# Summing the adjacency counts on VectorE before TensorE multiplies them, in a two-layer graph network

## The chip, the cores and the metric

One core of a Trainium2 chip. The metric is the device time of one execution in microseconds (us); lower is better. The kernel before takes 321.08 us, the median of 3 runs (320.94 to 321.26).

## What is computed

625 nodes of 512 features, 10000 edges (`src`, `dst`, each of one of 3 relations), nodes of 3 types. Layer 0 sums a message per edge, layer 1 is attention along the same edges with 8 heads of 64:

```python
h = maximum(layernorm(x), 0)
xr = einsum('nd,rde->rne', h, W_rel)
agg = segment_sum(xr[edge_type, src] + b_rel[edge_type], dst)
h_self = einsum('nd,tde->tne', h, W_self)[node_type, n] + b_self[node_type]
x = x + relu(h_self + agg)
h = maximum(layernorm(x), 0)
Q, K, V = split(h @ W_qkv.T + b_qkv)
att = softmax over the edges into each node of (Q[dst] . K[src]) / 8
x = x + segment_sum(att * V[src], dst) @ W_ff.T + b_ff
```

Two things are needed of the edges besides the messages: how many edges of each relation end in each node (the bias `b_rel` is added once for each), and, for the attention, how many edges run from each source to each target, whatever the relation (a pair with none is masked, and one with several gets the logarithm of their number).

## The kernel before, in words

The nodes are padded to NP = 640, five tiles (NT) of 128. The edges become a dense matrix of counts, `adjT[source in tile, source tile jt, relation r, target]`, fp16. It is built in 20 windows of 32 targets: VectorE (DVE) makes one-hot rows, `row_hot` (line 827) and `key_hot` (line 820), TensorE (PE) multiplies them (line 1083), and ScalarE (ACT) copies the window to `adjT` (line 523). Beside the windows runs a pipe for the self term (lines 1124 and 1130).

Then PE follows one list, `schedule`, written out by hand; ACT and DVE follow the same list, each doing its part of every unit in it. Units that use one of three PSUM banks in turn form the `ring`: a unit waits until DVE has freed the bank of the unit three places ahead of it (`take_bank`, semaphore `s_ufree`). The units around the change:

- `cnt`, two, one for each half of 320 target columns. PE writes the node types with 3 small matmuls (line 1162) and adds the counts by relation, 15 matmuls of 320 columns (line 1172): `sel6` sums over the sources within a tile, the 15 matmuls over tiles and relations. DVE copies the result to `cnt6` (lines 873 and 874), which meets the biases at line 1275.
- `z`, eight for each relation (4 groups of features, 2 halves): adjacency times features, 10 matmuls of 320 columns (line 1185). ACT takes the high part to `zT_even` or `zT_odd` (line 566), DVE the low part from the same bank (line 879) and frees it.
- `gemm`, five for each relation: 12 matmuls with `w_hl`, the two-part weights (line 1239).
- `m`, two for each target tile: `adjT` is turned over by multiplying it with an identity, 15 matmuls of 128 columns for a tile (line 1202), 12 in the first unit (4 source tiles, 512 columns) and 3 in the second (1 tile, 128 columns), which also sums over the relations. DVE makes `mcount` and `mask_add` (lines 893 and 895), ACT the logarithm (line 619), GpSimd (POOL) subtracts it (line 468).

The order is: `cnt` twice, `z` of relation 0, `z` of relation 1, then five times (`gemm` of relation 0, `m`, `m`), `z` of relation 2, the other gemms, the second layer.

Where a window needs over 16 chunks of edges (`pe.If(widest > EXACT16 // EL)`), counts may not fit fp16, and matmuls with the rest `adjT_res` are done too. With these edges the branch is skipped; its instructions are in the program.

ACT rounds the weights of relation 0, `w_hl` (line 514, `weights_hi`), after the last window, those of relation 1 ahead of its part of the first `z` unit of relation 1; POOL then makes the low parts, four operations each (line 439, `weights_lo`), and between the two it issues five gathers (line 457).

## Time and profile before

| | us |
|---|---|
| median of 3 runs | 321.08 |
| the profiled execution's own time | 321.26 |
| its span, first to last instruction | 319.5 |
| PE busy | 294.4 (92%) |
| DVE busy | 194.0 (61%) |
| ACT busy | 142.9 (45%) |
| POOL busy | 69.8 (22%) |

The granted TensorE clock is 1.00 of full speed (2.4 GHz) throughout. The chain that ended last is put down to PE for 81% of the span and to DVE for 12%. The windows fill the first 81 us, the stretch of `cnt` and the first 16 `z` units is 81 to 107.6 us, the gemms with `m` 107.6 to 126.7 us.

A duration in a row is the time an instruction is seen on its engine; two instructions of one engine overlap by a little, so that the distance from start to start is shorter.

### The profile page before, as it was taken

To read this page: it belongs to the slowest core of one execution; us is meant where nothing else is said; L and a number is where in the kernel's file an instruction comes from. 1 tells how busy PE (TensorE), PEld (TensorE's weight loads), DVE (VectorE), ACT (ScalarE), POOL (GpSimd) and SP (SyncE) were. 2 spreads that over 40 slices of the span, in tenths; PEclk is the share of its full clock that TensorE was granted. 3 is DMA by queue.
4 is the path that set the end of the run, shared out by engine and by line. 5 is a ranking of instruction groups with operands and counts; after the bars stand their busy time and mean duration, and the time that the engine had idled before them with its cause. 6 is when DMAs were issued, how large, how long until landed. Compare 5 with 4: busy or idle time off the path is not lost.

```text
span 319.5 us, 5460 instructions
## 1 busy us (share of the span) xinstructions
PE 294.4 (92%) x2006; PEld 226.4 (71%) x2006; DVE 194.0 (61%) x471; ACT 142.9 (45%) x282; POOL 69.8 (22%) x97
## 2 busy tenths in 40 slices
PE   2848699999999999998999999997999999999994
PEld 1513345544677788687887889997888898888882
DVE  5899977986234344334359744967857565565721
ACT  1152234523325322533343505687876464665621
POOL 6045003210655044800012402310002020020202
PEclk9999999999999999999999999999999999999999
DMA  5753992111080300045300000000000000000000
GB/s 181 251 209 131 331 386 106 67 36 55 17 291 8 133 2 2 2 131 139 125 0 0 2 0 3 0 3 0 2 0 2 36 0 35 1 2 35 1 35 29
DMA packets 10970, 22.29 MB, mean 70 GB/s; under 512 B 950, under 2 KB 966, under 8 KB 10938
## 3 DMA queue, kind: packets, MB, share of 16 engines
q1 hardware_dynamic: 8772, 16.80, 15.3%
q0 software_dynamic: 800, 2.62, 2.2%
q10 hardware_dynamic: 1366, 2.45, 2.1%
q8 instruction: 20, 0.33, 0.4%
q14 instruction: 12, 0.10, 0.1%
HBM read 15.60 MB, written 6.26 MB: 68 GB/s over the span
## 4 chain that ended last, share of the span: by engine, by line
PE 81%; DVE 12%; ACT 3%; issue 2%; DMA 1%; DVEq 0%; POOL 0%
PE banks L1239 15%; PE banks L1185 9%; PE banks L1225 9%; PE banks L1325 8%; PE banks L1130 8%; PE banks L1311 7%; PE banks L1300 7%; PE banks L1083 5%; PE banks L1345 5%; DVE key_hot L820 3%; DVE row_hot L827 2%; PE banks L1215 2%; PE banks L1335 2%; PE banks L1172 1%; PE banks L1202 1%
## 5 line engine op out<-in xcount | busy, mean ns | idle before, releaser
L1003 DVE CUSTOM_DVE_ANT_0 s_sb<-banks,mask_add 128x640 f32<-128x640 f32 x40 | 32.6, 822 | 22.2 <-PE banks L1300 22.1
L1083 PE MATMUL banks<-key_hot,row_hot 128*128 128x480 f16 x120 | 32.5, 419 | 9.0 <-DVE key_hot L820 9.0
L660 ACT ACTIVATE p_sb<-s_sb,neg_max 128x640 f32<-128x640 f32 x40 | 32.9, 823 | 17.3 <-DVE neg_max L1003 17.3
L820 DVE TENSOR_SCALAR key_hot<-iota,picked 128x480 f16<-128x480 f16 x120 | 36.9, 374 | 0.0
L1185 PE MATMUL banks<-adjT,h 128*128 128x320 f16 x240 | 33.1, 299 | 0.4 <-DVE zT_even L879 0.4
L1083 PEld LDWEIGHTS banks<-key_hot,row_hot 128*128 128x128 f16 x120 | 12.6, 105 | 26.4 <-DVE key_hot L820 9.2
L1185 PEld LDWEIGHTS banks<-adjT,h 128*128 128x128 f16 x240 | 23.3, 98 | 9.8 <-DVE zT_even L879 0.7
L1311 PE MATMUL banks<-ident,p_sb 128*128 128x128 f32 x200 | 29.6, 275 | 0.2 <-ACT pT L667 0.2
L490 POOL TENSOR_TENSOR msgT<-msg_f,msgT 128x128 fp32r<-128x128 f32 x20 | 8.6, 458 | 95.7 <-ACT msgT L681 95.7
L1239 PE MATMUL banks<-w_hl,zT_even 128*128 128x512 f32 x120 | 29.2, 394 | 0.0
L1300 PE MATMUL banks<-k_hi,q_st 128*128 128x320 f32 x80 | 27.1, 348 | 2.0 <-DVE neg_max L1003 2.0
L1225 PE MATMUL banks<-h2T,wqkvT 128*128 128x320 f32 x192 | 28.3, 309 | 0.0
L1225 PEld LDWEIGHTS banks<-h2T,wqkvT 128*128 128x128 f32 x192 | 28.2, 188 | 0.1
L1325 PE MATMUL banks<-pT,v_sb 128*64 128x128 f32 x400 | 26.0, 277 | 0.0
L1130 PE MATMUL banks<-w_self,hsT 128*128 x56 | 25.3, 594 | 0.5 <-ACT hsT L594 0.5
L1311 PEld LDWEIGHTS banks<-ident,p_sb 128*128 128x128 f32 x200 | 23.5, 141 | 2.9 <-issue 1.9
L1239 PEld LDWEIGHTS banks<-w_hl,zT_even 128*128 128x128 f32 x120 | 22.3, 188 | 4.4
L1325 PEld LDWEIGHTS banks<-pT,v_sb 128*64 128x64 f32 x400 | 21.5, 137 | 4.0 <-issue 3.8
L1300 PE MATMUL banks<-k_lo,q_st 128*128 128x320 f32 x80 | 24.0, 308 | 0.0
L827 DVE TENSOR_TENSOR row_hot<-iota,picked_row 128x768 f16<-128x768 f16 x20 | 19.0, 951 | 7.2 <-PE banks L1083 7.2
L523 ACT ACTIVATE adjT<-banks 128x480 f16<-128x480 f32 x20 | 11.4, 570 | 26.0 <-PE banks L1083 25.5
L667 ACT ACTIVATE pT<-banks 128x512 f32<-128x512 f32 x25 | 14.6, 586 | 14.5 <-PE banks L1311 14.5
(176 smaller groups left out, 466.4 us busy)
## 6 DMA issues: line engine op xcount, KB each, us to landing
w_self<-in_L_gnn_W_self_dram SPq DMA_DIRECT2D x3, 1024.0 KB, 9.4
raw<-in_L_gnn_W_rel_dram SPq DMA_DIRECT2D x3, 1024.0 KB, 15.6
raw<-in_L_gnn_W_qkv_dram SPq DMA_DIRECT2D x3, 1024.0 KB, 5.3
sorted_rows<-zero_rows ACTq DMA_DIRECT2D x1, 1792.0 KB, 10.7
self_rows<-hs SPq DMA_DIRECT2D x7, 256.0 KB, 2.0
hs<-sorted_rows SPq DMA_DIRECT2D x1, 1280.0 KB, 7.2
xs<-in_x_dram SPq DMA_DIRECT2D x1, 1024.0 KB
raw<-in_L_gnn_W_ff_dram SPq DMA_DIRECT2D x1, 1024.0 KB
```

Source lines behind the costliest of these rows:

```text
L660: nc.scalar.activation(p_sb[:, n % NPR, :], s_sb[:, n % NS, :], ACT.Exp, scale=-1.0, bias=neg_max[:, it, h:h + 1], accum_out=denom[:, it, ...
L820: return nc.vector.tensor_scalar(to_key, iota[:], float(KEYS * w), key, ALU.add, ALU.is_equal)
L827: nc.vector.tensor_tensor(row_hot[:, par], iota[:, 0:P].unsqueeze(1).broadcast_to([P, G, P]), picked_row[:, w * G:(w + 1) * G].unsqueeze(2 ...
L1003: nc.vector.tensor_tensor_reduce(s_sb[:, n % NS, :].rearrange("p (a j) -> p a j", a=2), banks[:, c:c + 2, 0:HALF], mask_add[:, it, :].rear ...
L1083: mm(banks[:, w % 2, 0:KEYS], row_hot[:, w % 2, k, :], key_hot[:, w % 2, k, :], start=(k == 0), stop=True, skip_group_check=True).then_inc ...
L1130: ins = mm(pipe_bank(u), hsT[:, t % 4, kt, :], w_self[:, bass.ds(offsets[t] + kt * D, D)], start=(kt == 0), stop=(kt == KD - 1))
L1185: ins = mm(b[:, 0:HALF], h16[:, p, jt, feats], adj[:, jt, r, cols], start=(start and n == 0), stop=(stop and n == len(pick) - 1), skip_gro ...
L1225: ins = mm(b[:, 0:HALF], wqkvT[:, pw, kt, o:o + P], h2T[:, ph, kt, half * HALF:(half + 1) * HALF], start=(n == 0), stop=(n == 3 * KD - 1))
L1239: ins = mm(to, lhs[:, pl, kt, it * P:(it + 1) * P], weights[:, pw, kt, c0:c0 + cn], start=(start and n == 0), stop=(n == 3 * KD - 1), skip ...
L1300: ins = mm(banks[:, 2 * (n % 2) + half, 0:HALF], q_st[:, h, it * P:(it + 1) * P], k[:, h, cols], start=(p == 0), stop=(p == 1))
L1311: ins = nc.tensor.transpose(banks[:, 5 + n % 2, i * P:(i + 1) * P], p_sb[:, h % NPR, jt * P:(jt + 1) * P], ident[:])
L1325: ins = mm(banks[64 * hh:64 * hh + 64, 4, a * P:(a + 1) * P], v_sb[:, jt, h * DK:(h + 1) * DK], pT[:, s, :], start=(jt == 0), stop=(jt == ...
```

## The change

- `col_sum[source in tile, relation, target]` is the sum of `adjT` over the five source tiles: four DVE additions of 1920 fp16 elements for a partition. Each follows DVE's part of one of the first four `z` units of relation 0.
- The two `cnt` units move behind the eight `z` units of relation 0. They multiply `col_sum`: 3 matmuls each in place of 15. They wait for the four additions.
- `rel_sum[source in tile, source tile, target]` is the sum over the relations: two DVE additions of 3200 fp16 elements, after DVE's part of the first two `z` units of relation 1.
- The `m` units turn `rel_sum` over: 5 matmuls for a target tile in place of 15, split 3 and 2 tiles (384 and 256 columns) in place of 4 and 1.
- The waits for the finished adjacency (`s_adj`, `s_whole`) go from the first `cnt` to the first `z` unit.
- In the branch that these edges skip, the sums are taken away again (`less6`, `less16`) and all counts and rests are added. POOL fills these constants at the start, 5 instructions more.

```diff
-        schedule = [("cnt", 0, 0), ("cnt", 1, 0)] + z_units(0) + z_units(1)
+        schedule = []
+        for n, u in enumerate(z_units(0)):
+            schedule += [u] + [("add", n)] * (n < NT - 1)
+        schedule += [("cnt", 0, 0), ("cnt", 1, 0)]
+        for n, u in enumerate(z_units(1)):
+            schedule += [u] + [("add", NT - 1 + n)] * (n < R - 1)
...
         def m_cols(part):
-            return (0, 4 * P) if part == 0 else (4 * P, P)
+            return (0, 3 * P) if part == 0 else (3 * P, 2 * P)
...
+            nc.gpsimd.memset(less6[:], 0.0).then_inc(s_fill, 1)
+            nc.gpsimd.tensor_scalar(less16[:], ident[:], -1.0, None, ALU.mult).then_inc(s_fill, 1)
+            pool.wait_ge(s_fill, FILLS + 1)
+            for r in range(R):
+                nc.gpsimd.memset(less6[:, r, r:BROWS:BG], -1.0).then_inc(s_fill, 1)
...
+                elif u[0] == "add":
+                    n = u[1]
+                    if n < NT - 1:
+                        into, one, two = col_sum[:], col_sum[:] if n else adjT[:, 0], adjT[:, n + 1]
+                        if n:
+                            dve.wait_ge(s_add, n)
+                    else:
+                        into, two = rel_sum[:], adjT[:, :, n - NT + 2, :]
+                        one = adjT[:, :, 0, :] if n == NT - 1 else rel_sum[:]
+                        dve.wait_ge(s_add, n)
+                    if n == 0:
+                        dve.wait_ge(s_adj, NW)
+                    nc.vector.tensor_tensor(into, one, two, ALU.add).then_inc(s_add, 1)
...
                     if half == 0:
-                        pe.wait_ge(s_adj, NW)
-                        pe.wait_ge(s_whole, 1)
                         pe.wait_ge(s_keys, MASKS)
-                        pe.wait_ge(s_fill, FILLS)
+                        pe.wait_ge(s_fill, FILLS + 2 + R)
+                        pe.wait_ge(s_add, NT - 1)
...
                     for r in range(R):
-                        for jt in range(NT):
-                            ins = mm(b[0:BROWS, 0:HALF], sel6[:, r, :], adjT[:, jt, r, cols], start=False,
-                                     stop=(r == R - 1 and jt == NT - 1), skip_group_check=True)
+                        ins = mm(b[0:BROWS, 0:HALF], sel6[:, r, :], col_sum[:, r, cols], start=False,
+                                 stop=(r == R - 1), skip_group_check=True)
                 elif kind == "z":
...
                     if (r, dt, half) == (0, 0, 0):
+                        pe.wait_ge(s_adj, NW)
+                        pe.wait_ge(s_whole, 1)
                         pe.wait_ge(s_h16lo, NT)
...
                     _, it, part = u
-                    tiles = range(4) if part == 0 else range(4, NT)
...
-                    add(adjT, items[:-1], True, False)
+                    tiles = range(3) if part == 0 else range(3, NT)
+                    if u == ("m", 0, 0):
+                        pe.wait_ge(s_add, NT + R - 2)
+
+                    def flip(n, counts, sign, start=False, stop=False):
+                        return mm(b[:, n * P:(n + 1) * P], counts[:, it * P:(it + 1) * P], sign[:], start=start,
+                                  stop=stop, skip_group_check=True)
+                    for n, jt in enumerate(tiles[:-1]):
+                        flip(n, rel_sum[:, jt], ident16, start=(n == 0))
                     with pe.If(widest > EXACT16 // EL):
...
+                    ins = flip(len(tiles) - 1, rel_sum[:, tiles[-1]], ident16, stop=True)
```

DVE's order after the last window, before:

```order
L873 CAST cnt<-banks 70x320
L874 TENSOR_TENSOR cnt<-banks,cnt 6x320
L873 CAST cnt<-banks 70x320
L874 TENSOR_TENSOR cnt<-banks,cnt 6x320
L879 TENSOR_TENSOR zT_even<-banks,zT_even 128x320 x8
L879 TENSOR_TENSOR zT_odd<-banks,zT_odd 128x320 x8
L893 TENSOR_SCALAR mcount<-banks 128x512
```

and in the changed kernel, where line 895 is what 879 was and line 1018 is the addition:

```order
L895 TENSOR_TENSOR zT_even<-banks,zT_even 128x320
L1018 TENSOR_TENSOR col_sum<-adjT 128x1920
L895 TENSOR_TENSOR zT_even<-banks,zT_even 128x320
L1018 TENSOR_TENSOR col_sum<-col_sum,adjT 128x1920
L895 TENSOR_TENSOR zT_even<-banks,zT_even 128x320
L1018 TENSOR_TENSOR col_sum<-col_sum,adjT 128x1920
L895 TENSOR_TENSOR zT_even<-banks,zT_even 128x320
L1018 TENSOR_TENSOR col_sum<-col_sum,adjT 128x1920
L895 TENSOR_TENSOR zT_even<-banks,zT_even 128x320 x4
L889 CAST cnt<-banks 70x320
L890 TENSOR_TENSOR cnt<-banks,cnt 6x320
```

DVE frees a bank with each `zT` instruction, and in the first four units an addition now stands between one freeing and the next. The two additions to `rel_sum` stand in the same way behind the first two `zT_odd` instructions.

PE's order at the end of a `cnt` unit, before (the rows between the two branch rows are skipped; `h_59` is `h16`):

```order
L1165 COMPARE_AND_BRANCH
L1168 MATMUL banks<-adjT_res,sel 70x320 x15
L1165 UNCONDITIONAL_BRANCH
L1172 MATMUL banks<-adjT,sel 70x320 x15
L1185 MATMUL banks<-adjT,h_59 128x320 x9
```

and in the changed kernel, the end of the second `cnt` and the start of relation 1:

```order
L1193 UNCONDITIONAL_BRANCH
L1202 MATMUL banks<-col_sum,sel 70x320 x3
L1217 MATMUL banks<-adjT,h_59 128x320 x9
L1222 COMPARE_AND_BRANCH
L1217 MATMUL banks<-adjT_res,h_59 128x320 x10
```

The 15 matmuls of a `cnt` unit have become 3, and the unit stands between the relations, no longer ahead of both.

## Rows read from the trace of the kernel before

**Rows 1.** Busy time by stretch: us, each engine, clock, DMA share, GB/s.

```profile
81.00:86.00 5.00, 4.87 (x39) 3.99 (x40) 1.10 (x3) 1.83 (x2) 3.10 (x3) 1.00 0.03 7
86.00:97.00 11.00, 11.00 (x83) 7.92 (x82) 4.20 (x9) 3.21 (x8) 6.63 (x7) 1.00 0.60 215
...
108.00:127.00 19.00, 19.00 (x142) 15.49 (x141) 7.49 (x18) 5.10 (x10) 6.85 (x8) 1.00 0.03 11
```

**Rows 2.** The chain that ended last, 76 to 112 us: start, us, what.

```profile
80.42 0.71 issue
81.13 0.30 PE banks L1162 x3
81.43 2.22 PE banks L1172 x15
83.65 0.15 PE banks L1162 x3
83.80 2.04 PE banks L1172 x15
85.84 21.73 PE banks L1185 x160
...
110.57 0.85 PE banks L1202 x15
```

**Rows 3.** Timeline, ACT, DVE and POOL: start, us, instruction, idle before.

```profile
80.92 1.90 ACT L514 ACTIVATE w_hl<-raw 128x2048 fp32r<-128x2048 f32 x1
82.90 4.94 POOL L439 TENSOR_TENSOR w_hl<-raw,w_hl 128x512 fp32r<-128x512 f32 x4 [17.99 <-ACT w_hl L514]
87.23 0.44 ACT L566 ACTIVATE zT_even<-banks 128x320 fp32r<-128x320 f32 x1 [4.41 <-PE banks L1185]
87.77 0.49 DVE L879 TENSOR_TENSOR zT_even<-banks,zT_even 128x320 fp32r<-128x320 f32 x1 [0.89 <-ACT zT_even L566]
...
99.05 4.96 POOL L439 TENSOR_TENSOR w_hl<-raw,w_hl 128x512 fp32r<-128x512 f32 x4 [5.05 <-ACT w_hl L514]
```

**Rows 4.** Groups by line and shape, DVE: out<-in, busy us, mean ns.

```profile
L827 DVE TENSOR_TENSOR row_hot<-iota,picked_row 128x768 f16<-128x768 f16 x20 | 19.0, 951 | 7.2 <-PE banks L1083 7.2
...
L893 DVE TENSOR_SCALAR mcount<-banks 128x512 f32<-128x512 f32 x5 | 3.5, 692 | 11.4 <-PE banks L1202 11.4
...
L893 DVE TENSOR_SCALAR mcount<-banks 128x128 f32<-128x128 f32 x5 | 1.4, 281 | 0.0
```

**Rows 5.** Single lines, DVE: ns min/median/max, first and last start.

```profile
L820 DVE TENSOR_SCALAR key_hot<-iota,picked x120: 319/337/1244, 10.2 to 77.9; 128x480 f16<-128x480 f16 x120
...
L923 DVE CAST k_hi<-qk_f x8: 484/608/898, 194.9 to 206.8; 64x640 fp32r<-64x640 f32 x8
```

**Rows 6.** Timeline 51 to 61 us, DVE against POOL.

```profile
52.43 1.24 DVE L820 TENSOR_SCALAR key_hot<-iota,picked 128x480 f16<-128x480 f16 x1
...
52.21 2.47 POOL L451 TENSOR_TENSOR h<-in,h 128x512 f16<-128x512 f32 x2 [3.77 <-ACT h L544]
...
58.48 0.95 DVE L827 TENSOR_TENSOR row_hot<-iota,picked_row 128x768 f16<-128x768 f16 x1
58.51 1.94 POOL L451 TENSOR_TENSOR h<-in,h 128x512 f16<-128x512 f32 x1 [3.83 <-ACT h L544]
```

**Rows 7.** The chain that ended last, 126 to 138 us.

```profile
128.02 0.21 DVE mcount L893
...
128.47 1.90 ACT w_hl L514
...
131.34 6.96 PE banks L1185 x50
```

**Rows 8.** Timeline 0 to 22 us: POOL's last fill, its next work, a held DVE row.

```profile
3.04 1.16 DVE L700 TENSOR_SCALAR tiles_i<-edges_i 80x125 int32<-80x125 int32 x1
...
6.18 0.17 POOL L435 MEMSET sel<- 128x3 f16 x3
...
19.84 1.17 POOL L447 DMA_INDIRECT sorted_rows<-in,place_u  x1 [13.49 <-ACT in L539]
```

More of the change, by code:

```diff
@@ L166, in gnn_kernel @@
         zero_rows = place("zero_rows", o_ss, [P, D], F32)
+        col_sum = place("col_sum", o_r4 + 47232, [P, R, NP], F16)
+        rel_sum = place("rel_sum", o_r4 + 51072, [P, NT, NP], F16)
+        less6 = place("less6", o_r4 + 61760, [P, R, BROWS], F16)
+        less16 = place("less16", o_r4 + 62208, [P, P], F16)
         mlog = place("mlog", o_r4 + 43136, [P, 2, 512], F32)
@@ L234, in gnn_kernel @@
         s_ufree = sem("s_ufree")
+        s_add = sem("s_add")
         s_gemm = sem("s_gemm")
@@ L287, in gnn_kernel @@
         schedule += [("q", a, half) for a in range(KD) for half in range(2)]
-        ring = [u for u in schedule if u[0] not in ("gemm", "sum", "ln")]
+        ring = [u for u in schedule if u[0] not in ("gemm", "sum", "ln", "add")]
         number = {u: n for n, u in enumerate(ring)}
@@ L633, in _ @@
                     continue
-                if u[0] in ("gemm", "sum"):
+                if u[0] in ("gemm", "sum", "add"):
                     continue
@@ L1166, in unit @@
                         for r in range(R):
+                            mm(b[0:BROWS, 0:HALF], less6[:, r, :], col_sum[:, r, cols], start=False, stop=False,
+                               skip_group_check=True)
                             for jt in range(NT):
-                                mm(b[0:BROWS, 0:HALF], sel6[:, r, :], adjT_res[:, jt, r, cols], start=False,
-                                   stop=False, skip_group_check=True)
+                                for adj in (adjT, adjT_res):
+                                    mm(b[0:BROWS, 0:HALF], sel6[:, r, :], adj[:, jt, r, cols], start=False,
+                                       stop=False, skip_group_check=True)
                     for r in range(R):
-                        for jt in range(NT):
-                            ins = mm(b[0:BROWS, 0:HALF], sel6[:, r, :], adjT[:, jt, r, cols], start=False,
-                                     stop=(r == R - 1 and jt == NT - 1), skip_group_check=True)
+                        ins = mm(b[0:BROWS, 0:HALF], sel6[:, r, :], col_sum[:, r, cols], start=False,
+                                 stop=(r == R - 1), skip_group_check=True)
                 elif kind == "z":
@@ L1195, in unit @@
                     _, it, part = u
-                    tiles = range(4) if part == 0 else range(4, NT)
-                    items = [(r, jt) for jt in tiles for r in range(R)]
-                    def add(adj, pick, start, stop):
-                        for n, (r, jt) in enumerate(pick):
-                            rows = (jt - tiles[0]) * P
-                            ins = mm(b[:, rows:rows + P], adj[:, jt, r, it * P:(it + 1) * P], ident16[:],
-                                     start=(start and n == 0), stop=(stop and n == len(pick) - 1),
-                                     skip_group_check=True)
-                        return ins
-                    add(adjT, items[:-1], True, False)
-                    with pe.If(widest > EXACT16 // EL):
-                        add(adjT_res, items, False, False)
-                    ins = add(adjT, items[-1:], False, True)
+                    tiles = range(3) if part == 0 else range(3, NT)
[6 more added lines that the diff above has]
+                        flip(n, rel_sum[:, jt], ident16, start=(n == 0))
+                    with pe.If(widest > EXACT16 // EL):
+                        for n, jt in enumerate(tiles):
+                            flip(n, rel_sum[:, jt], less16)
+                            for r in range(R):
+                                flip(n, adjT[:, jt, r], ident16)
+                                flip(n, adjT_res[:, jt, r], ident16)
+                    ins = flip(len(tiles) - 1, rel_sum[:, tiles[-1]], ident16, stop=True)
                 elif kind == "wt":
@@ L1262, in _ @@
             for u in schedule:
-                if u[0] in ("sum", "ln"):
+                if u[0] in ("sum", "ln", "add"):
                     continue
```

## Prediction

> **What bounds the kernel now.** The page first: PE is busy for 92% of the span and holds 81% of the chain, so work taken off PE can shorten the run. The busy time by stretch [rows 1] says so for the place itself: from 86 to 97 us PE is busy for 11.00 of 11.00 us while DVE works 4.20 and ACT 3.21; from 108 to 127 us it is the same. The granted clock is 1.00 in each stretch, the upper level (2.4 GHz).
>
> The chain [rows 2] gives the prices. From 81.13 to 85.84 us, 4.71 us, PE does the two `cnt` units: small matmuls of 0.30 and 0.15 us, and two runs of 15 in 2.22 and 2.04 us. The 16 `z` units follow in 21.73 us with no gap, 1.36 us each, or 0.136 us for a matmul. An `m` pair is 15 matmuls in 0.85 us, 0.057 us each, and there are five pairs.
>
> The timeline [rows 3] shows the path of one unit: PE ends at about 87.20, ACT works 87.23 to 87.67, DVE 87.77 to 88.26, then the bank is free. That is 1.06 us behind PE's end, and with three banks PE needs it only after two more units, 2.7 us. So there are 1.65 us of slack for each bank, and DVE needs 0.49 of every 1.36 us. The additions must live in that.
>
> **Term 1, `cnt`: less 3.6 us.** 24 of 30 matmuls go. What is left, at the pace of an unbroken run, is 0.15 + 3 x 0.136 = 0.56 us for a unit, 1.12 for both; 4.71 - 1.12 = 3.59 us. All of it was on the chain.
>
> **Term 2, `m`: less 2.8 us.** 50 of 75 matmuls go, 50 x 0.057 = 2.83 us. A skipped branch now stands among fewer instructions. I cost it at nothing: the old second `m` unit had only 2 matmuls between branches and its pair still ran at 0.057 us, and in the first `cnt`, where PE had just been waiting, the first matmul behind the branch came 0.30 us after the masks' first [rows 2]. The upper bound is 0.2 us for a pair, 1 us in all, and a gain is excluded. DVE's two shapes are 384 and 256 columns in place of 512 and 128; between 692 and 281 ns [rows 4] they come to 0.56 and 0.42 us, twice each, 1.95 us for a pair as before. With a pair and its gemm now every 3.3 us on PE they stay covered.
>
> **Term 3, the additions.** DVE gets four operations of 1920 and two of 3200 elements, which nothing in the trace resembles exactly. The nearest rows from above: `row_hot`, also fp16 with two SBUF inputs, takes 951 ns for 768 elements; with 692 ns for 512 and 281 for 128 [rows 4] that is 1.05 ns an element and 0.15 us fixed, so 2.15 and 3.5 us. From below: `key_hot`, fp16 with one stream, 480 elements in 319 ns [rows 5], 0.35 ns an element, so 0.8 and 1.3 us. I take half of `row_hot`'s rate, 0.52 ns, which the `k_hi` cast shows (640 in 484 ns [rows 5]): `row_hot` repeats one element of its inputs over a row while the additions read packed fp16 as `key_hot` does, so they lie nearer `key_hot`, but they stream two inputs where it streams one. That makes 1.15 and 1.82 us, and 0.07 less from start to start. The rate of `row_hot` stays as a rival.
>
> By itself an addition and a `z` part would take 1.5 us of DVE for each 1.36 us of PE for four units, which the slack covers; the two of 1.82 us take it just about. **But POOL works at the same time.** `weights_lo` of relation 0 runs from 82.90, four operations in 4.94 us, pitch 1.24 [rows 3]. What the two engines do to each other is in [rows 6]: the `key_hot` that starts at 52.43, with POOL inside an operation from 52.21, takes 1.24 us in place of 0.32 and ends at 53.67, just after POOL's first of two operations; it is let in between them. And at 58.48 `row_hot`, an operation with two SBUF inputs, runs its usual 0.95 us, while POOL's operation that starts 0.03 us later takes 1.94 us where two take 2.47: it was held for 0.7 us. So a DVE operation with two SBUF inputs and a POOL operation that reads SBUF exclude each other, at least when DVE is first. I take it to hold both ways, with turns. The Trainium skill (SBUF — State Buffer, Who interferes with whom) states just that, "A DVE instruction with two SBUF inputs contends with a GpSimd instruction that reads SBUF", and the second to issue waits for the first to end; by it the sum is the one below, by a reading that lets an addition run beside POOL it is the first rival. The trace agrees for DVE first (1.94 against 1.24 us); POOL first is in no row.
>
> Worked through on the clock of the trace, `z` now starting at 81.13:
> - ACT still rounds the weights until 82.82 [rows 3], so the first `z` part comes at 82.86 and DVE's at 83.4. POOL starts at 82.9. The first addition wants 83.85, is held to 84.18, ends 85.26; POOL's second operation follows to 86.5; and so on in turns of 2.3 us (1.08 + 1.24). The additions end at 85.3, 87.6, 89.9 and 92.2.
> - DVE's part of the second to fifth unit comes behind each, so the banks fall free at 85.7, 88.0, 90.35 and 92.7. PE's sixth unit starts at 88.1 in place of 87.9, the seventh 1.0 later still, the eighth 0.95. PE loses 2.1 us. `cnt` then finds its sums ready.
> - POOL ends `weights_lo` at about 91, not 87.8, issues the gathers until 97.3, and starts the second `weights_lo` there (99.05 before [rows 3], and ACT's rounding is done at about 96.4). The two additions of 1.82 us take turns with it: 98.6 to 100.3 and 101.6 to 103.3. PE's fifth unit of relation 1 is 0.2 late, the sixth 1.6. PE loses 1.8 us.
> Term 3 is 3.9 us. The later weights on POOL have slack: they are needed at 107 and 138 us.
>
> **Term 4, the start: 0.1 us.** POOL's fills end at 6.35 and its next work comes 13.49 us later [rows 8], so five more fills cost POOL nothing. DVE's chain of small operations runs beside them; such a one was held at 3.04 us for 1.16 us [rows 8]. I take 0.1, between 0 and 0.5.
>
> **Term 5, behind the `m` units: nothing.** PE stops there until 131.34 because ACT rounds the third weights (1.90 us) after the last logarithm [rows 7]. This hangs on the `m` units' DVE and ACT parts, whose last logarithm is 256 columns in place of 128 but starts earlier; within 0.1 us it moves along with PE.
>
> **Sum.** -3.6 - 2.8 + 3.9 + 0.1 = -2.4 us. The profiled execution took 321.26 us itself, so 318.9; it lies 0.18 above the median, and against 321.08 the forecast is 318.7 us. The end of the first 16 `z` units stays where it is (107.57 before, about 107.9 after), and the gain is that of `m`.
>
> **The rivals.**
> 1. *POOL doesn't hold the additions.* For it: no row shows POOL first against two SBUF inputs. Against it: the 0.7 us at 58.5 us [rows 6]. Term 3 shrinks to 0.1, and the sum is -6.2: 314.9 us. The lower price of an addition (0.8 and 1.3 us), even with turns, leads to about 0.8 for term 3 and 315.6 us.
> 2. *POOL keeps its turn.* If POOL's next operation goes ahead of a waiting addition, the first one waits for all four, until 87.8, and the next for the second set: term 3 becomes 7.4 us, the sum +1.1: 322.2 us. Against it: `key_hot` at 52.43 was let in after one. One lost turn costs 1.24 us, 319.9.
> 3. *The additions run at `row_hot`'s rate*, one element in 1.04 ns, and DVE becomes the bound of the stretch; this is the one that ends slower. DVE then needs 2.07 + 0.46 us for a unit, over the 1.36 us of PE; it decides from where the sum of four such excesses passes the slack of 1.65 us, at about 1.3 us for an addition. Without holding, term 3 is 6.8 us and the sum +0.4: 321.5 us. With POOL's turns it is 10.4 and the sum +4.0: 325.1 us. For it: every operation with two tensors in the trace goes at that rate, `row_hot` in fp16 among them. The Trainium skill (VectorE: DVE Perf Modes, the perf-mode tier table) speaks against it: fp16 additions from SBUF run two elements a cycle where all steps are one, 1224 ns for 2048, which by its formula would be 1.16 and 1.82 us. No row here shows that; `row_hot` has repeated elements and so agrees with neither more.
> 4. *The change doesn't do what it says*: the branch is taken, or the skipped code of 33 instructions in `cnt` costs a fetch. The trace has 30 matmuls of line 1172 and none with `adjT_res`, so it is skipped, and 180 rows skipped after the last window hide in the 0.71 us of waiting for ACT [rows 2]. Then a gain of only 1 us is left, or none: about 320.5 us.
>
> **How the numbers follow.** Forecast 55%; rival 1, 22%; rival 2, 9%; rival 3, 10% (4 without and 6 with turns); rival 4, 4%. The range reaches from rival 1, a little below for a first `z` unit without start-up loss, 314.6, to 321.0, which takes in one lost turn, the 0.5 us of the start and half of the branch bound. Outside lie rival 3, most of rival 2 and a few per cent of tails, together just under 2 in 10. The forecast's own range is 317.6 to 320.3. A measurement here tells 0.2%, 0.64 us, from no change. Faster: forecast, rival 1 and some of 4, 0.79. Same: rival 3 without turns and the rest of 4, 0.06. Slower: 0.15.
>
> **What would show it.** In the changed profile: the additions 1.15 us by themselves but seen 1.2 to 2.4 us long while POOL works; POOL's `weights_lo` spread over 8 us in place of 4.9; gaps of PE before `z` units, released by DVE, of 3.9 us together; `cnt` in 1.1 us; the end of the 16th `z` unit near 107.9; an `m` pair in 0.28 us; all later steps 2.4 us earlier. The forecast is wrong if the additions take over 2 us with POOL idle (rival 3), if they overlap POOL's operations at full speed (rival 1), or if the first ends only at 89 us (rival 2).

## The result, and the profile after

The changed kernel takes 323.05 us (median of 7 runs, 322.11 to 324.12) against 321.26 us of the kernel before in the same session (7 runs, 320.94 to 321.69). The ratio is 1.0054, with a 95% interval of 1.0035 to 1.0073: slower by 0.5%. The forecast was 318.7 us, 0.7% faster, in a range of 314.6 to 321.0. The profiled execution took 322.55 us, 1.3 more than that of before. The seven executions differ in the granted clock of TensorE (PE), which is 0.989 on the mean in the longest (324.12 us) and 0.995 in the profiled one.

The chain of waits of the changed kernel, 80 to 133 us, answers to [rows 2, 7] (start, us, what, with the rows that bear on nothing here left out, as in the timelines below; L1217 is now the `z` matmul, L1202 the sums of `cnt`, L1233 the `m` matmul, L895 DVE's part of `z`, L1018 the additions):

```profile
81.33 5.61 PE banks L1217 x40
...
93.83 0.14 PE banks L1190 x3
93.97 0.41 PE banks L1202 x3
...
94.96 1.55 PE banks L1217 x10
...
97.56 0.82 DVE rel_sum L1018
98.38 5.89 issue
104.27 0.49 DVE zT_odd L895
...
104.81 6.91 PE banks L1217 x40
111.72 0.24 PE banks L1309
...
114.69 0.30 PE banks L1233 x5
...
129.90 1.89 ACT w_hl L530
...
132.77 2.35 PE banks L1217 x16
```

This gives the account between two marks. A `z` unit without loss is 1.358 us (21.73 / 16 [rows 2]).

- The start: the first unit behind the windows begins at 81.33 in place of 81.13, +0.20. That is not clear of chance: in the profiles of kernels with the same start it begins anywhere from 80.93 (`pad_pool`) to 82.73 us (`wait_rel`).
- `cnt`: 93.83 to 94.96 is 1.13 us in place of 4.71, -3.58.
- Relation 0: its eight units take 12.50 us (81.33 to 93.83) in place of 10.87, +1.63.
- Relation 1: eight units take 16.76 us (94.96 to 111.72), +5.90. Of these, 4.42 lie before the fifth unit (104.81, due at 100.39), and 1.48 in the last four, which take 6.91 us in place of 5.43.
- Together +4.15, and the 16th unit does end at 111.72 in place of 107.57.
- From there to the third relation's matmuls it is 21.05 us in place of 23.77, -2.72: an `m` pair is 0.30 us in place of 0.85, and the stall behind it is the same as in [rows 7].

The 5.89 us of "issue" are time for which the profile names no releaser; the timeline below shows the held addition in it. What is left at the third relation is +1.43, of which 1.3 arrives at the end of the profiled execution.

The timeline of the changed kernel shows relation 0 (82.9 to 92.3 us) and relation 1 (96.7 to 104.9 us), against [rows 3] (start, us, instruction, idle time before it and what ended that):

```profile
83.11 7.71 POOL L455 TENSOR_TENSOR w_hl<-raw,w_hl 128x512 fp32r<-128x512 f32 x4 [17.99 <-ACT w_hl L530]
83.87 1.53 DVE L1018 TENSOR_TENSOR col_sum<-adjT 128x1920 f16<-128x1920 f16 x1
85.72 1.82 DVE L1018 TENSOR_TENSOR col_sum<-col_sum,adjT 128x1920 f16<-128x1920 f16 x1
...
90.15 1.53 PE L1217 MATMUL banks<-adjT,h 128*128 128x320 f16 x10 [0.51 <-DVE zT_even L895]
...
92.30 1.53 PE L1217 MATMUL banks<-adjT,h 128*128 128x320 f16 x10 [0.61 <-DVE zT_even L895]
...
96.77 0.94 POOL L473 DMA_INDIRECT self_sum<-self_rows,place_u  x1 [0.30 <-issue]
...
97.47 6.88 DVE L1018 TENSOR_TENSOR rel_sum<-adjT 128x3200 f16<-128x3200 f16 x1
97.73 4.93 POOL L455 TENSOR_TENSOR w_hl<-raw,w_hl 128x512 fp32r<-128x512 f32 x4
...
104.68 1.81 DVE L1018 TENSOR_TENSOR rel_sum<-rel_sum,adjT 128x3200 f16<-128x3200 f16 x1
...
104.81 1.51 PE L1217 MATMUL banks<-adjT,h 128*128 128x320 f16 x5 [4.25 <-DVE zT_odd L895]
```

In relation 0 the two engines take turns: POOL's four operations are spread over 7.71 us, and the additions are seen 1.53 and 1.82 us long. In relation 1 they don't: POOL's four run in their usual 4.93 us, and the addition, which asked 0.26 us *before* the first of them, ends 1.69 us after the last (104.35 against 102.66), which is its own duration (1.81). DVE is in order, so its part of `z` stands behind the addition, the banks stay full, and PE idles 4.25 us.

The busy time by stretch of the changed kernel adds what the granted clock did:

```profile
100.00:105.00 5.00, 0.75 (x6) 0.32 (x4) 5.00 (x3) 0.44 (x1) 2.66 (x3) 0.91 0.18 53
105.00:107.00 2.00, 2.00 (x9) 1.14 (x8) 2.00 (x3) 0.00 (x0) 0.00 (x0) 0.50 1.00 389
107.00:110.00 3.00, 3.00 (x22) 2.08 (x21) 1.20 (x3) 0.88 (x2) 0.00 (x0) 0.92 0.03 10
```

From 105 to 107 us PE is busy for all 2.00 us and the granted clock is 0.50, the lower of its two levels (1.2 GHz): 9 matmuls start in 2 us, where 22 start in the next 3. PE had idled 4.25 us just before. By an estimate from these rows the half clock costs 2.00 x 0.50 = 1.0 us there and 3.00 x 0.08 = 0.24 in the row below, most of the 1.48 us that the last four units are late.

### The profile page after: what moved, and what is told of

Its sections match the earlier page's. It is cut to its first block, busy times and chain, and to the rows that moved or that the text cites. A ratio compares the mean times of both kernels' runs of the same rounds, so it can differ in the third digit from the quotient of the medians.

```text
span 320.8 us, 5326 instructions
## 1 busy us (share of the span) xinstructions
PE 290.3 (90%) x1932; PEld 221.1 (69%) x1932; DVE 208.4 (65%) x477; ACT 143.0 (45%) x282; POOL 75.5 (24%) x102
## 4 chain that ended last, share of the span: by engine, by line
PE 76%; DVE 13%; issue 4%; ACT 3%; DMA 2%; POOL 0%; DVEq 0%
PE banks L1273 14%; PE banks L1259 9%; PE banks L1359 8%; PE banks L1159 8%; PE banks L1345 7%; PE banks L1217 7%; PE banks L1334 7%; PE banks L1112 6%; PE banks L1379 5%; DVE key_hot L836 3%; DVE row_hot L843 2%; DMA raw<-in_L_gnn_W_qkv_dram 2%; PE banks L1369 2%; PE banks L1249 1%; PE banks L1153 1%
## 5 line engine op out<-in xcount | busy, mean ns | idle before, releaser
L1217 PE MATMUL banks<-adjT,h 128*128 128x320 f16 x240 | 35.1, 306 | 6.5 <-DVE zT_odd L895 4.2
L1217 PEld LDWEIGHTS banks<-adjT,h 128*128 128x128 f16 x240 | 23.5, 100 | 18.0 <-DVE zT_odd L895 4.6
L455 POOL TENSOR_TENSOR w_hl<-raw,w_hl 128x512 fp32r<-128x512 f32 x12 | 17.6, 1498 | 18.8 <-ACT w_hl L530 18.8
```

The source lines that it names most:

```text
L1217: ins = mm(b[:, 0:HALF], h16[:, p, jt, feats], adj[:, jt, r, cols], start=(start and n == 0), stop=(stop and n == len(pick) - 1), skip_gro ...
```

## The experiments

"Before" is the kernel before in the same session; the ratio is to it.

**The hold: let POOL wait (wait_rel).** POOL's `weights_lo(1)` waits until both additions of the mask are done, so that these four operations can't hold them.

```diff
+            pool.wait_ge(s_add, NT + R - 2)
             for kt in range(KD):
                 weights_lo(1, kt)
```

> The changed kernel, but POOL waits for both additions to rel_sum before its weights_lo of relation 1. Theory (the hold): in the changed kernel the first of these additions took 6.88 us because POOL's four operations ran from 97.7 to 102.7 and kept it out, and PE then stood still for 4.25 us and lost 1.5 us more at the lower clock level. Both additions then take 1.8 us, PE has no gap over 0.5 us in relation 1, the clock stays at 1.00 there, and the run is 5.5 to 6 us shorter than the changed kernel: about 317.3 us. Rival (DVE load): two additions of 1.8 us are too much for DVE by themselves; then most of the 5.9 us stays, 321 us or more.

Measured: 317.26 us (316.76 to 318.39), before 321.31, ratio 0.9869 (0.9853 to 0.9886). That is 5.8 us below the changed kernel, the 5.90 of the account. Timeline of this kernel, 96 to 108 us:

```profile
96.35 11.17 PE L1218 MATMUL banks<-adjT,h 128*128 128x320 f16 x80
98.17 0.94 POOL L473 DMA_INDIRECT self_sum<-self_rows,place_u  x1 [0.30 <-issue]
98.87 1.81 DVE L1019 TENSOR_TENSOR rel_sum<-adjT 128x3200 f16<-128x3200 f16 x1
101.00 1.81 DVE L1019 TENSOR_TENSOR rel_sum<-rel_sum,adjT 128x3200 f16<-128x3200 f16 x1
102.90 4.96 POOL L455 TENSOR_TENSOR w_hl<-raw,w_hl 128x512 fp32r<-128x512 f32 x4 [3.79 <-DVE rel_sum L1019]
```

All 80 matmuls of relation 1 run without a gap beside additions of 1.81 us. So in this relation it is not the additions' own time that costs anything, but their wait for POOL. The first addition asks 0.70 us into POOL's last gather, just as in the changed kernel (97.47 against 96.77), and takes its own 1.81 us: the gather doesn't hold it, only the four operations behind it do.

**One half of the change each (cnt_only, m_only).** The first keeps the sums over source tiles and the reordered `cnt`, with `m` as before. The second keeps the sums over relations, with `cnt` first as before.

```diff
 cnt_only:
-            schedule += [u] + [("add", NT - 1 + n)] * (n < R - 1)
+            schedule += [u]
...
 m_only:
-        for n, u in enumerate(z_units(0)):
-            schedule += [u] + [("add", n)] * (n < NT - 1)
-        schedule += [("cnt", 0, 0), ("cnt", 1, 0)]
+        schedule = [("cnt", 0, 0), ("cnt", 1, 0)] + z_units(0)
```

> Only the cnt half of the change: four additions to col_sum, cnt behind relation 0; the m units as before, no rel_sum. Theory (the hold): -3.6 us for 24 matmuls, +1.6 us for turns between additions and POOL, +0.2 for the start: 1.8 us faster than before, 319.4 us. Rival (moving cnt costs by itself, through ACT's weights or the start of z): no faster than before, 321 us.

> Only the m half: cnt as before and in front, two additions to rel_sum in relation 1. POOL's weights_lo of relation 1 here start at about 99.0, before the first addition asks (about 99.8), so the addition meets a running TENSOR_TENSOR and not a gather. If what matters is what POOL is doing when the addition asks (arrival), it is let in after one operation, as the additions to col_sum were: -2.7 + 1.8 us, 320.3 us. If the shape matters (3200 elements in strided pieces of 640), it is kept out for all four, until 104, and PE stops for about 4 us and loses the clock: +3 us, 324.3 us.

Measured: `cnt_only` 319.71 us (319.21 to 320.89), ratio 0.9958 (0.9945 to 0.9971); the account has -3.58 + 1.63 + 0.20 = -1.75 us for this half, and -1.60 came. `m_only` 321.06 us (320.57 to 322.32), ratio 0.999 (0.9973 to 1.0006). Its timeline, 99 to 106 us:

```profile
99.29 8.12 POOL L452 TENSOR_TENSOR w_hl<-raw,w_hl 128x512 fp32r<-128x512 f32 x4 [5.07 <-ACT w_hl L527]
100.05 2.19 DVE L1015 TENSOR_TENSOR rel_sum<-adjT 128x3200 f16<-128x3200 f16 x1
102.57 2.49 DVE L1015 TENSOR_TENSOR rel_sum<-rel_sum,adjT 128x3200 f16<-128x3200 f16 x1
102.70 1.53 PE L1211 MATMUL banks<-adjT,h 128*128 128x320 f16 x10 [0.33 <-DVE zT_odd L892]
105.51 3.71 PE L1211 MATMUL banks<-adjT,h 128*128 128x320 f16 x26 [1.28 <-DVE zT_odd L892]
```

The same addition in the same relation takes turns with POOL here, and PE's gaps are 1.61 us with the clock at 1.00. Here the turns of the prediction happened. Between the marks of the account this half has +0.24 at the start, +1.95 in relation 1 and -2.71 behind it, together -0.52; -0.25 came in the medians, so the 320.3 us expected with turns were not reached. Neither half alone is slower than before; together they are.

**The additions exchanged (swap).** The two of `m` go into relation 0 and the four of `cnt` into relation 1, with `cnt` behind its sixth unit, to see whether shape or place is held.

```diff
+            schedule += [u] + [("add", n)] * (n < R - 1)
...
+            schedule += [u] + [("add", R - 1 + n)] * (n < NT - 1)
+            if n == 5:
+                schedule += [("cnt", 0, 0), ("cnt", 1, 0)]
```

> The changed kernel with the places of the additions exchanged: the two to rel_sum behind the first two z units of relation 0, the four to col_sum behind the first four of relation 1, cnt behind the sixth. Arrival: the first addition to rel_sum asks at 83.9 during POOL's first operation, is let in after it and ends at about 86.2; the first to col_sum asks during the gathers or just before weights_lo of relation 1 and is kept out by all four, over 5 us long. Shape: the first to rel_sum is kept out until 88.0 and takes about 6 us, the ones to col_sum take 1.2 to 2.0 us each. Both theories give about 322 to 323.5 us in all; the durations tell them apart.

Measured: 321.08 us (319.4 to 322.79), ratio 0.9987 (0.9963 to 1.0011). The additions of 3200 elements take 2185 and 2487 ns in relation 0, by turns. Relation 1 in the timeline of this kernel:

```profile
96.46 0.95 POOL L474 DMA_INDIRECT self_sum<-self_rows,place_u  x1 [0.30 <-issue]
96.71 1.15 DVE L1020 TENSOR_TENSOR col_sum<-adjT 128x1920 f16<-128x1920 f16 x1
97.43 7.98 POOL L456 TENSOR_TENSOR w_hl<-raw,w_hl 128x512 fp32r<-128x512 f32 x4
98.17 1.83 DVE L1020 TENSOR_TENSOR col_sum<-col_sum,adjT 128x1920 f16<-128x1920 f16 x1
...
104.43 0.30 PE L1192 MATMUL banks<-ident,mask 128*70 128x128 f16 x3 [2.44 <-DVE col_sum L1020]
```

An addition that asks early in a gather runs at once, in its own 1.15 us; POOL's first operation, starting under it, has to wait, and from then on they take turns. No addition is held for long in either relation; each theory was right for one of them, and both had forecast 322 to 323.5 us. The clock falls here too: behind the gap of 2.44 us it is 0.50 from 106 to 109 us. The times of the ten executions go with it: the same kernel took 319.4 and 319.51 us where the mean granted clock was 1.000, 320.64 to 321.73 (six) at 0.995, and 322.2 and 322.79 at 0.989.

**The moment at which the addition asks (pad_dve, pad_pool, pad_dve4, pad_dve6).** The hold could be a close race at POOL's start. Small reductions on DVE ahead of the first addition of relation 1 move it later, two small memsets on POOL ahead of `weights_lo(1)` move POOL later. Their results are used by nothing.

```diff
 pad_dve (pad_dve4 and pad_dve6 have four and six, into another buffer):
+                    if n == NT - 1:
+                        nc.vector.tensor_reduce(chunk_mm[:, 0:1], edges_i[:, 1, :], AX.X, ALU.min)
+                        nc.vector.tensor_reduce(chunk_mm[:, 1:2], edges_i[:, 1, :], AX.X, ALU.max)
...
 pad_pool, ahead of weights_lo(1):
+            nc.gpsimd.memset(edge_keys[:, 0, :], 0.0)
+            nc.gpsimd.memset(edge_keys[:, 1, :], 0.0)
```

> The changed kernel with two small reductions of 0.27 us (their results are unused) on DVE ahead of the first addition to rel_sum, so that it asks about 0.4 us later, at 97.9, when POOL's first weights_lo of relation 1 (from 97.7) is under way and no longer at the same moment. If the long hold came from asking at the very moment POOL goes from the last gather to four operations in a row, the addition is now let in after one of them, as in the run with only the m half: 2.2 to 2.6 us long, PE waits about 1.5 us in place of 4.25, the clock stays at 1.00, about 319 us. If a gather just before is what matters, it is still held for over 6 us, 323 us or more.

> The changed kernel with two small memsets on POOL ahead of its weights_lo of relation 1, so that these start about 0.3 us later, at about 98.0, and the addition to rel_sum (97.5) is clearly first. By the theory of the close tie the addition takes 1.8 to 1.9 us, POOL's first operation is the one that is held, and the run takes 318 to 319 us. If the order of asking does not matter, the addition is held for over 6 us again, 323 us.

> Part of the changed kernel moved: four small VectorE reductions (0.19 us from start to start; their results are used by nothing) stand ahead of the first addition of relation 1, which so asks about 0.5 us after POOL's first of four operations has begun (0.26 us before it in the changed kernel, 0.12 after it with two reductions). Theory moment: an addition that asks while a POOL operation is well under way is let in behind that one, as in relation 0, where it asked 0.78 us after; then it takes 1.8 + 0.7 = 2.5 us, PE's gap is about 1.6 us and the clock stays at 1.00: about 320.5 us. Theory place: in this place of the program, behind the gathers, POOL keeps all four whatever the moment: the addition takes 4.93 - 0.5 + 1.7 = 6.1 us, PE's gap stays at 4.2 us, about 323 us. If the gate lies between, this run is held and the one with six is not.

> The same with six reductions: the first addition of relation 1 asks about 0.9 us after POOL's first operation has begun, as late in it as in relation 0 (0.78) and in the run with the additions of m alone (0.76). Theory moment: it is let in behind the first operation and takes 1.8 + 0.4 = 2.2 us, the second 2.5; PE's gaps are about 0.6 and 1.3 us, clock 1.00: 320.0 us. Theory place: held for all four again, 5.7 us, 323 us.

Measured, with the start of the addition against that of POOL's first operation:

| run | us | addition asks | addition takes | PE's gap |
|---|---|---|---|---|
| pad_pool | 322.99 (10 runs) | 0.50 us before | 7.12 us | 4.49 us |
| changed kernel | 323.05 (7) | 0.26 before | 6.88 | 4.25 |
| pad_dve | 323.12 (10) | 0.12 after | 6.50 | 4.25 |
| pad_dve4 | 323.94 (1) | 0.48 after | 6.14 | 4.27 |
| pad_dve6 | 323.18 (5) | 0.87 after | 5.75 | 4.26 |

In each, POOL's four operations run in 4.93 or 4.94 us and the addition ends 1.68 or 1.69 us behind them. A close race would have given the addition 2.2 to 2.6 us in `pad_dve` and 1.8 to 1.9 in `pad_pool`; that theory fell. The moment alone has no say: in `m_only` the addition asked 0.76 us after POOL's start and had its turn, in `pad_dve6` 0.87 after and had not.

**The size of the addition (split).** The first addition of relation 1 in a piece of 1920 and one of 1280 elements.

```diff
+                    if n == NT - 1:
+                        nc.vector.tensor_tensor(into[:, 0:3], one[:, 0:3], two[:, 0:3], ALU.add)
+                        into, one, two = into[:, 3:NT], one[:, 3:NT], two[:, 3:NT]
```

> The changed kernel with the first addition of relation 1 in two pieces, source tiles 0 to 2 (1920 elements, the size of an addition of cnt, which was never held for more than one operation) and 3 to 4 (1280). Theory size: the long operation is what is kept out; the piece of 1920 is let in within 1.3 us, 2.5 us at most, and the time falls to about 320. Theory place: the first piece is held for all four, 6.3 us, and the time stays at 323. In either case the pieces by themselves take 1.15 and 0.8 us.

Measured: 323.89 us (one run); the piece of 1920 takes 6.22 us, that of 1280 right behind it 0.81. The size has no say either.

**POOL's wait (gap, early_lo, bridge).** In the runs with turns, the row of POOL's four operations carries a bracket, such as [5.07 <-ACT w_hl L527] in `m_only`: POOL had been waiting when the first began. Relation 1 of `swap` is the exception: no bracket, but an addition was already running when POOL's first operation began. In the held runs there is none: the four follow the gathers at once. `gap` adds ten reductions to DVE and a short wait to POOL; `bridge` has the same ten, and 20 small memsets in place of the wait; `early_lo` puts `weights_lo(1)` ahead of the gathers, where it has to wait for ACT.

```diff
 gap, with ten reductions ahead of the first addition:
+            pool.wait_ge(s_uhi, act_done[("z", 1, 0, 1)])
             for kt in range(KD):
                 weights_lo(1, kt)
...
 bridge, the same with
+            for k in range(20):
+                nc.gpsimd.memset(edge_keys[:, 1, 4 * k:4 * k + 4], 0.0)
...
 early_lo:
+            for kt in range(KD):
+                weights_lo(1, kt)
             pool.wait_ge(s_kept, 16 * SORTED)
             for it in range(NT):
```

> The changed kernel with ten small VectorE reductions ahead of the first addition of relation 1 (used by nothing), and POOL's weights_lo(1) waiting for ACT's part of the second unit of relation 1, so that POOL idles about 1 us behind its last gather and starts near 98.7 us; the addition asks near 99.8, 1 us after. Theory gap: POOL gives up the port only where its run of operations began from a wait, as in relation 0 and in the runs with turns; then the addition takes about 2.1 us and the second 2.5, and the clock stays at 1.00: 320 us. Theory place: in this relation with the gathers ahead it is held for the rest of the four whatever comes before, 5.7 us: 323.5 us.

> The changed kernel with POOL's five gathers and its weights_lo(1) exchanged: POOL waits for ACT's rounding (done at 96.1), starts its four operations from a wait near 96.2, and the gathers come after. The addition asks at 97.5, 1.3 us after. Theory gap: turns, 1.8 to 2.6 us for each addition, PE's gaps 1.8 us together in relation 1, the clock at 1.00: 319.2 us. Theory place: with the gathers gone from ahead it is let in too, by the same numbers. Theory that the addition itself (3200 elements, two strided inputs, right behind a part of z) is what loses against POOL here: held until 101.1 us, 5.3 us; PE's gap about 2.5 us: 321 us. The gathers behind cost nothing before the sums that read them, or up to 1 us if they come too late.

> The changed kernel with ten small VectorE reductions ahead of the first addition of relation 1 (used by nothing), as in the run that let POOL wait, but POOL's wait replaced by 20 small memsets (used by nothing) between its last gather and weights_lo(1). POOL so starts the four operations about 1 us behind the gather, near 98.8, as there, but without having waited. The addition asks near 99.5 to 99.8. Theory: a run of POOL operations that follows other POOL work without a stop keeps the port; the addition is held for the rest of the four, 5 us or more, PE's gap is over 4 us, and the time 323 to 324 us. Rival: what decides is that a gather lies just ahead of the run; with 1 us between them the addition is let in within 1.3 us, takes 1.8 to 2.6 us, and the time is 319.7 us, as with the wait.

Measured: `gap` 319.69 us (one run), `early_lo` 318.66 us (318.57 to 318.87, ratio 0.9908, 0.9872 to 0.9943), `bridge` 323.62 us (323.21 to 324.16, ratio 1.0071, 1.0054 to 1.0088). The timeline of `gap`:

```profile
99.19 8.43 POOL L455 TENSOR_TENSOR w_hl<-raw,w_hl 128x512 fp32r<-128x512 f32 x4 [1.40 <-ACT zT_odd L583]
99.43 1.81 DVE L1022 TENSOR_TENSOR rel_sum<-adjT 128x3200 f16<-128x3200 f16 x1
101.56 2.48 DVE L1022 TENSOR_TENSOR rel_sum<-rel_sum,adjT 128x3200 f16<-128x3200 f16 x1
```

That of `early_lo`:

```profile
96.23 8.12 POOL L455 TENSOR_TENSOR w_hl<-raw,w_hl 128x512 fp32r<-128x512 f32 x4 [5.36 <-ACT w_hl L530]
97.52 2.88 DVE L1018 TENSOR_TENSOR rel_sum<-adjT 128x3200 f16<-128x3200 f16 x1
```

And that of `bridge`:

```profile
97.76 0.71 POOL L477 MEMSET edge_keys<- 128x4 f32 x20
98.41 4.93 POOL L455 TENSOR_TENSOR w_hl<-raw,w_hl 128x512 fp32r<-128x512 f32 x4
99.41 5.61 DVE L1023 TENSOR_TENSOR rel_sum<-adjT 128x3200 f16<-128x3200 f16 x1
105.48 0.98 PE L1222 MATMUL banks<-adjT,h 128*128 128x320 f16 x3 [4.88 <-DVE zT_odd L897]
```

With a wait of 1.40 us ahead, POOL's four are stretched to 8.43 us and the additions take 1.81 and 2.48; with other POOL work in that place they are not stretched and the addition is held for 5.61. The theory of the place falls, since `gap` has the same place behind the gathers. The moment doesn't explain it either: the addition in `gap` asks 0.24 us into the run of four, between `pad_dve` (0.12) and `pad_dve4` (0.48), which were both held, and that in `early_lo` 1.29 us into it, later than the 1.00 of `bridge`. What separates all these runs is whether POOL had been waiting when its four operations began.

One rival is left. In `bridge` the four begin only 0.65 us behind the end of the last gather (97.76 to 98.41), less than the 1 us meant and the 1.40 of `gap`. A rule by the time since the last gather, with its bound between 0.65 and 1.40 us, would fit every run here, and memsets of 1.4 us or more would have had to test it. The runs don't show what in the engines makes the difference.

**Later additions, POOL untouched (late_rel).**

```diff
-            schedule += [u] + [("add", NT - 1 + n)] * (n < R - 1)
+            schedule += [u] + [("add", NT - 1 + n - 4)] * (4 <= n < R + 3)
```

> The two additions of relation 1 stand behind its fifth and sixth unit instead of its first and second; nothing else is changed and POOL waits for nothing. DVE then asks for the first at about 102.5 us, when POOL's weights_lo (97.7 to 102.7) is at its end. Both theories of the hold expect it let in at once or within 0.3 us: 1.8 to 2.1 us each, PE's gap at most 0.4 us in relation 1, the clock at 1.00, and 317.3 us (the changed kernel less 5.9 us of relation 1, plus 0.2), like the run in which POOL waited. If something other than POOL's operations in that stretch is what costs the time, it stays near 323.

Measured: 316.8 us (316.6 to 317.02), ratio 0.9859 (0.9844 to 0.9874). POOL's four run from 97.53 to 102.47, the additions start at 102.70 and 104.84 and take 1.82 and 1.81 us, and PE has no gap in relation 1. Moving two entries of the order by four units is worth as much as the wait.

**The best version (wait_both, best, wait_fill).** `wait_both` lets POOL wait in both relations: for the four additions before `weights_lo(0)`, for all six before `weights_lo(1)`. `best` starts two additions before the first unit, has all six in relation 0, lets POOL wait for all six before `weights_lo(0)`, and moves POOL's fills behind its scatter. `wait_fill` is `wait_both` with the fills moved alone.

```diff
 wait_both:
+            pool.wait_ge(s_add, NT - 1)
             for kt in range(KD):
                 weights_lo(0, kt)
...
+            pool.wait_ge(s_add, NT + R - 2)
             for kt in range(KD):
                 weights_lo(1, kt)
...
 best:
+        schedule += [("add", 0), ("add", 1)]
+            schedule += [u] + [("add", {0: 2, 1: 3, 4: 4, 6: 5}.get(n))] * (n in (0, 1, 4, 6))
+        schedule += [("cnt", 0, 0), ("cnt", 1, 0)] + z_units(1)
```

> POOL waits for the four additions to col_sum before weights_lo of relation 0 and for the two to rel_sum before those of relation 1. All additions unheld: 1.15 and 1.8 us; the turns in relation 0 (1.6 us of PE) go too. 317.3 - 1.6 = 315.7 us. If the turns cost PE nothing by themselves (DVE's own load does), 317.3 us as with the one wait.

> Two additions to col_sum right behind the last window, ahead of DVE's first z part, where DVE is idle; the two others behind the first two z units; the two to rel_sum behind the fifth and seventh unit of relation 0; POOL waits for all six before weights_lo of relation 0; POOL's five new fills behind the scatter. PE should then run from 81.2 to about 104.1 us without a gap: -3.6 - 2.7 us against before, 315.0 us. If a wait is left somewhere (POOL's late weights, the gathers), it shows as a gap of PE before 127 us or a time over 316 us.

> POOL waits for the additions in both relations, and POOL's fills for cnt (five more than before) stand behind the scatter instead of at the start, where the small DVE operations of lines 729 to 733 were late by some 0.06 us beside them. Theory: the start is on the chain, so the run is 0.1 to 0.2 us shorter than with the waits alone (315.33): 315.2 us. Rival: the start is bound by the transfers that follow, and it stays at 315.3. PE without a gap from the first z unit to its last in either.

Measured: `wait_both` 315.33 us (315.16 to 315.54), ratio 0.9801 (0.9769 to 0.9833); `best` 316.11 us (315.95 to 317.5), 0.9841 (0.98 to 0.9883); `wait_fill` 315.57 us (315.27 to 315.68), 0.9815 (0.9802 to 0.9828). The timeline of `wait_both`:

```profile
81.32 11.03 PE L1219 MATMUL banks<-adjT,h 128*128 128x320 f16 x80 [0.71 <-issue]
83.86 1.15 DVE L1020 TENSOR_TENSOR col_sum<-adjT 128x1920 f16<-128x1920 f16 x1
...
89.49 4.96 POOL L455 TENSOR_TENSOR w_hl<-raw,w_hl 128x512 fp32r<-128x512 f32 x4 [24.38 <-DVE col_sum L1020]
...
93.47 11.17 PE L1219 MATMUL banks<-adjT,h 128*128 128x320 f16 x80
...
95.99 1.81 DVE L1020 TENSOR_TENSOR rel_sum<-adjT 128x3200 f16<-128x3200 f16 x1
97.15 1.47 POOL L474 DMA_INDIRECT self_sum<-self_rows,place_u  x1 [0.30 <-issue]
98.13 1.81 DVE L1020 TENSOR_TENSOR rel_sum<-rel_sum,adjT 128x3200 f16<-128x3200 f16 x1
98.93 1.83 POOL L474 DMA_INDIRECT self_sum<-self_rows,place_u  x1 [0.30 <-issue]
```

PE runs both relations without a gap, the six additions take their own time, and POOL's weights are in place when PE needs them. It beats both kernels, 6.1 us under before. `best` was no better: the addition at 91.74 us came just ahead of DVE's last part of relation 0, and PE idled 0.79 us. It had been expected at 315.0 us. `wait_fill` was a miss too: the matmuls with `pick` came back to 7.28 us (7.33 in the changed kernel, 7.27 before), and nothing of that arrived at the end.

## Why the prediction was wrong

**Term 1, `cnt`, -3.6 us: right.** 1.13 us against a worked-out 1.12.

**Term 2, `m`, -2.8 us: right.** -2.72 by the marks; a pair is 0.30 us where 0.28 was forecast, and the skipped branch costs at most the 0.02. DVE's two shapes take 558 and 415 ns in the changed kernel, against the 0.56 and 0.42 interpolated between [rows 4].

**Term 3, the additions, +3.9 us: wrong, it is +7.5.** Three of its steps held. The price of an addition by itself, 1.15 and 1.82 us by half of `row_hot`'s rate, is what `wait_both` shows (1.15 and 1.81), so rival 3 falls. The tier table of the Trainium skill that the prediction cites there (VectorE: DVE Perf Modes) agrees: by the prediction's working from it, 1.16 and 1.82. The turns in relation 0 came nearly as worked out, with two delays of PE instead of three, 1.63 us in place of 2.1. The forecast also had POOL's second `weights_lo` begin at 97.3 (97.73 came), behind the gathers.

The step that failed is "The two additions of 1.82 us take turns with it". In relation 1 POOL kept its four operations ahead of the waiting addition: 4.42 us by that, and 1.48 more, almost all for the half clock that followed PE's idle time. That makes 5.90 in place of 1.8, and `wait_rel`, which takes this wait away, gives 5.8 us back. It is the mechanism of rival 2, which had it in both relations or neither and priced it at 7.4 us; with a chance of 9% it was not far off in time (322.2), for partly the wrong reason. The clock stood in no case at all.

Why it could be missed shows in [rows 6], the evidence for turns: both POOL rows there end in brackets, [3.77 <-ACT h L544] and [3.83 <-ACT h L544]. POOL had waited before each. So had it before `weights_lo` in [rows 3], 17.99 and 5.05 us. The prediction itself worked out that in relation 1 this wait would vanish, since the turns make POOL late and the rounded weights come early, but took the behaviour of a POOL that had waited over to one that comes straight from its gathers. No row of before shows that case. The rule of the Trainium skill (SBUF — State Buffer, Who interferes with whom) that the sentence leant on says who blocks whom for one instruction and nothing of who comes next; its sentence "Issue order, not op shape, decides who blocks" is borne out for the shape (`split`) and not, by the recorded starts, for the order. In relation 1 the addition began 0.26 us ahead of POOL's first operation, and 0.50 in `pad_pool`, though POOL was then still in its last gather, and was held; in `gap` it began 0.24 us behind and ran in its own 1.81 us. The measurement decides.

**Term 4, the start, +0.1 us: not contradicted, not shown.** 0.06 us is seen in the first 7.33 us, and nothing came of taking it away (`wait_fill`). The +0.20 at the first `z` unit is less than its spread between profiles.

**Term 5, nothing behind `m`: right.** PE's stall ends with ACT's third weights as in [rows 7].

**Rival 1** did not happen but can be built: with POOL kept away, `wait_both` gains 6.1 us where that rival said 6.2. The additions there never meet POOL's weight operations, so this bears out the rival's sum and not its mechanism. **Rival 4** falls: both branches are skipped.

## What to carry to other kernels

When work goes to VectorE in a stretch where GpSimd also works, the price is not the instruction's own duration but what it waits for, and an in-order engine hands that wait on to whatever stands behind it, here PE's banks. Before taking a pattern of turns from a trace, read what the other engine was doing just before its run began, above all whether it had been waiting, and whether that will still be so after the change. Where one engine has slack, spend it: a wait on GpSimd for the additions, or additions moved four units later, turned a loss of 1.8 us into gains of 4.1 to 6.1.

## What the runs showed of the hardware

- A VectorE addition with two SBUF inputs is held for all four of GpSimd's operations (5.6 to 7.1 us) when these follow other GpSimd work without a wait, and for at most 1.1 us, the operation under way or the next, when they began from a wait: seven kernels of the first kind (the changed one, the four with padding, `split`, `bridge`), three of the second in relation 1 (`m_only`, `gap`, `early_lo`), besides relation 0. It also gets its turns where it was running before GpSimd's first operation (`swap`). Whether the wait or the 1.4 us and more since the last gather decides is open.
- A gather issued by GpSimd doesn't hold an addition that asks in it (1.15 us in `swap`, 0.25 us into the gather; 1.81 in `wait_rel`, 0.70 into it), but one that begins under an addition is lengthened: 1.47 and 1.83 us in place of 0.95 in `wait_both`, each ending 0.82 us after the addition.
- After 4.25 us of idle time PE's granted clock was 0.50 for the next 2 us and more, in a kernel where it had been 1.00; after a gap of 2.44 us in `swap` it fell to 0.50 too, about 1.2 us behind the end of the gap; in the run with gaps of 0.33 and 1.28 us (`m_only`) it stayed at 1.00.
- An fp16 addition of two packed SBUF tensors on 128 partitions takes 1.15 us for 1920 elements and 1.81 for 3200, about half the time per element of `row_hot` [rows 4] (951 ns for 768), whose inputs repeat an element.
